# An adaLN block on one core: two row sums a head with six carried tiles, division inside the attention, a shorter preparation and a projection without GpSimd

## The reference, cut to what matters

```python
mod = (silu(c) @ wmod).reshape(B, 6, 1, -1)          # sa, ca, ga, sb, cb, gb; ga and gb kept away from 0
h = layernorm(x) * (1 + ca) + sa                     # x: 2 x 2048 x 512
mixed = h @ Wqkv.T                                   # q, k, v of 16 heads of 32, per batch: 32 heads
attn = softmax(q @ k.T * 32 ** -0.5)                 # 2048 x 2048 for each of the 32 heads
x = x + ga * ((attn @ v) @ Wproj.T + bproj)
h = layernorm(x) * (1 + cb) + sb
hidden = fwht(silu(h @ W1.T) * (h @ W3.T))           # 2048 wide
x = x + gb * (hidden @ W2.T)
```

## Time and profile before

| | us |
|---|---|
| median of three runs | 3419.07 (3417.18 to 3424.57) |
| the profiled execution, its own time | 3422.99 |
| its span, first to last instruction | 3421.2 |
| busy: PE, DVE, ACT, POOL | 3173.1, 1892.1, 1534.8, 1588.4 |
| prepare and entry of project_qkv, up to its first matmul | 109.5 |
| project_qkv, matmuls | 283.5 |
| attend, from the last projection to its first score | 67 |
| attend, 31 heads | 1607 |
| attend, last head, which sums by PE | 65 |
| gap to the first matmul of project_out | 25 |
| project_out | 186 |
| feed_forward | 1078 |

### The profile page before, as it was taken

How to read it: one execution, slowest core, us unless ns; L and a number is a source line. 1 busy time by engine, 2 the same in 40 slices (tenths; PEclk the granted TensorE clock), 3 DMA queues, 4 the chain that set the end, 5 groups by cost and what they waited for, 6 DMA issues and landing times. The chain is left out here.

```text
span 3421.2 us, 48695 instructions
## 1 busy us (share of the span) xinstructions
PE 3173.1 (93%) x15340; PEld 2114.3 (62%) x15340; DVE 1892.1 (55%) x3144; ACT 1534.8 (45%) x2869; POOL 1588.4 (46%) x566
## 2 busy tenths in 40 slices
PE   5899799999999999999999998667999999999998
PEld 3688555545555555545555552456888888888887
DVE  5443398778777777777777780653333233223232
ACT  3333146666666666656666665233322222222221
POOL 5000059999888998989989992540000000000000
PEclk7999879999999999999999999878999999999999
DMA  5556537877777777777777763854221121121111
GB/s 213 163 164 183 157 67 166 173 161 163 167 156 168 160 162 157 158 165 162 160 159 163 166 135 76 245 189 164 84 83 47 56 71 44 57 70 44 59 56 34
DMA packets 150990, 446.92 MB, mean 131 GB/s; under 512 B 27398, under 2 KB 45062, under 8 KB 116044
## 3 DMA queue, kind: packets, MB, share of 16 engines
q0 software_dynamic: 28064, 199.24, 28.9%
q1 hardware_dynamic: 122668, 244.39, 24.6%
HBM read 167.78 MB, written 80.23 MB: 72 GB/s over the span
## 5 line engine op out<-in xcount | busy, mean ns | idle before, releaser
L1009 DVE TENSOR_REDUCE mxp<-pmax 128x1 f32<-128x512 f32 x2048 | 1258.9, 681 | 373.3 <-PE pmax L830 372.8
L966 ACT ACTIVATE prob<-pexp 128x512 f32<-128x512 f32 x2048 | 1037.9, 623 | 576.5 <-PE pexp L875 491.0
L830 PE MATMUL pmax<-kst,qst 96*128 96x512 f32 x2048 | 870.7, 433 | 41.4 <-issue 21.0
L1066 POOL TENSOR_TENSOR gsum<-gsum,prob 128x2048 f32<-128x2048 f32 x186 | 877.6, 4718 | 17.9
L875 PE MATMUL pexp<-qst,kst 98*128 98x512 f32 x2048 | 827.9, 424 | 45.2 <-ACT prob L966 45.2
L830 PEld LDWEIGHTS pmax<-kst,qst 96*128 96x128 f32 x2048 | 407.7, 199 | 327.1 <-DVE mxp L1009 184.1
L875 PEld LDWEIGHTS pexp<-qst,kst 98*128 98x128 f32 x2048 | 399.8, 196 | 246.5 <-ACT prob L966 174.3
L1066 POOL TENSOR_TENSOR gsum<-prob 128x2048 f32<-128x2048 f32 x93 | 472.0, 5076 | 76.9 <-ACT prob L966 76.9
L884 PE MATMUL pctx<-prob,v 128*32 128x512 f32 x4096 | 498.2, 603 | 0.0
L1642 DVE TENSOR_TENSOR hid<-sil,pl 128x512 f32<-128x512 f32 x128 | 88.0, 688 | 638.6 <-PE pl L51 631.6
L51 PE MATMUL pg<-h2f,w 128*128 128x512 f32 x1536 | 371.1, 391 | 1.1 <-issue 1.1
(11 more groups left out here) (109 smaller groups left out, 1757.6 us busy)
## 6 DMA issues: line engine op xcount, KB each, us to landing
gsum<-prob POOLq DMA_DIRECT2D x124, 1024.0 KB, 9.7
gsum<-gsum POOLq DMA_DIRECT2D x62, 1024.0 KB, 8.5
w<-w_scratch SPq DMA_DIRECT2D x128, 256.0 KB, 2.6
qst<-q_scratch SPq DMA_DIRECT2D x96, 256.0 KB, 6.4
kst<-k_scratch SPq DMA_DIRECT2D x96, 256.0 KB, 7.2
xin<-in_L_attn_query_dram SPq DMA_DIRECT2D x16, 1024.0 KB, 8.5
q_scratch<-obq SPq DMA_DIRECT2D x32, 512.0 KB, 5.0
k_scratch<-obq SPq DMA_DIRECT2D x32, 512.0 KB, 3.6
```

The lines of the kernel that those rows point to most:

```text
L830: pe.matmul(pmax[:, bank, :], qst[0:KR, slot, qt * P:(qt + 1) * P], kst[0:KR, slot, kc * TOK:(kc + 1) * TOK], start=True, stop=True).then_ ...
L966: act.activation(prob[:, kt % RING, j * TOK:(j + 1) * TOK], pexp[:, score_bank(r, n), :], ACT.Exp, scale=SCALE).then_inc(exp_done, 1)
L1009: dve.tensor_reduce(mxp[:, par, u // QJ, u % QJ:u % QJ + 1], pmax[:, bank, :], X, ALU.max).then_inc(mx_done, 1)
L1066: pool.tensor_tensor(dst, a, prob[:, kt % RING, :], ALU.add).then_inc(add_done, 1)
```

## The change: what it does

- **Row sums.** Two buffers for a head instead of three, each kept for two heads. POOL does eight adds (tiles 0 to 4, and 5, 6, 8, 9, 11), six tiles (7, 10, 12, 13, 14, 15) are carried by DMA, to the buffers 0, 0, 1, 0, 1, 0, and nothing is merged: PE runs `unit` on both buffers, after the fifth burst.
- **Order.** `M` and `q` alternate strictly. `INVERT_AT` goes from 44 to 20. The loop over heads is written out on all engines.
- **Division.** SP broadcasts the reciprocals to `recb` and POOL multiplies the contexts of head g-2 in `divide`; SP stores them after that. The last head is divided by DVE, from PSUM. `project_out` loads no reciprocals any more.
- **Preparation.** The whole rows of Wqkv come in four transfers, nothing of W2 is done, low parts are made by DVE from PSUM, tokens of tile 0 are turned there. The transform of W2 goes into `project_qkv`: POOL loads a quarter and does 8 butterflies of 128x1024, PE turns 16 blocks and does 4 Hadamard matmuls, in tiles 0, 2, 4 and 6 (`fold_turn` after result 9, `fold_mult` after result 11).
- **project_out** has no POOL work: the bias is a two-row matmul at the end of each result.

```diff
+                load_rows(0)
+                load_rows(1)
+                load_tokens(sp, ins, keep["xin"], 0, 0).then_inc(keep["x_in"][0], 16)
+                load_rows(2)
+                load_rows(3)
+                load_mod(0)
+                load_mod(1)
+                sp.dma_start(natp[:, :, :], ins["wproj"].rearrange("(j p) n -> p j n", p=P)).then_inc(natp_in, 16)
+                load_mod(2)
+                load_mod(3)
+                sp.dma_start(had[:, :], ins["hadamard"]).then_inc(keep["had_in"], 16)
+                load_tokens(sp, ins, keep["xin"], 0, 1).then_inc(keep["x_in"][1], 16)
...
+                def fold_mult(s, b):
+
+                    n = FOLD_AT.index(2 * s + b)
+                    pe.wait_ge(keep["had_in"], 16)
+                    for i in range(DC):
+                        pe.wait_ge(w2_taken, DC * n + i + 1)
+                        pe.matmul(pt[:, i, :], had[:, :], wt[:, i * D:(i + 1) * D], start=True, stop=True).then_inc(w2_mm, 1)
...
+                for n in range(DC):
+                    if n:
+                        pool.wait_ge(w2_turned, DC * n)
+                    pool.dma_start(wn[:, :], ins["w2"][n * P:(n + 1) * P, :]).then_inc(w2_in, 16)
+                    if n:
+                        pool.wait_ge(w2_scaled, DC * n)
+                        pool.dma_start(scratch["w2"][:, :, (n - 1) * P:n * P].rearrange("c p n -> p c n"),
+                                       wt[:, :].rearrange("p (c n) -> p c n", c=HC)).then_inc(w2_out, 16)
+                        pool.wait_ge(w2_out, 16 * n)
+                    pool.wait_ge(w2_in, 16 * (n + 1))
+                    for m in range(2 * STAGES):
...
-ORDER = "MqMqMqMqMqMqqMqM"
-POOLED = ((0, 1, 2, 3), (5, 6, 7, 8), (11, 12, 13, 15))
-CARRIED = (4, 9, 10, 14)
-MERGES = 6
+ORDER = "Mq" * 8
+POOLED = ((0, 1, 2, 3, 4), (5, 6, 8, 9, 11))
+CARRIED = (7, 10, 12, 13, 14, 15)
+UNITS = len(POOLED)
 ADDS = sum(len(g) - 1 for g in POOLED)
-TURN_AFTER, UNIT_AFTER = 48, 55
-INVERT_AT = 44
+TURN_AFTER, UNIT_AFTER = 48, 39
+INVERT_AT = 20
...
-        late[UNIT_AFTER // 8].append(("unit", 0))
+        late[UNIT_AFTER // 8] += [("unit", k) for k in range(UNITS)]
...
+    CARRY_TO = (0, 0, 1, 0, 1, 0)
...
+                def spread_rec(g):
 
                     sp.wait_ge(inverted, g + 1)
-                    sp.dma_start(scratch["rec"][bass.ds(g, 1), :].rearrange("o (p n) -> (o p) n", p=P),
-                                 recc[:, par, :]).then_inc(rec_out[par], 16)
+                    sp.dma_start(scratch["rec"].rearrange("(p n) -> p n", p=P), recc[:, :]).then_inc(rec_out, 16)
+                    sp.wait_ge(rec_out, 16 * (g + 1))
+                    if g:
+                        sp.wait_ge(divided, g)
+                    for j in range(QJ):
+                        sp.dma_start(recb[j * HD:(j + 1) * HD, :], scratch["rec"][j * TOK:(j + 1) * TOK]
+                                     .partition_broadcast(HD)).then_inc(rec_in, 16)
 
...
-                    par = (r - 1) % 2
-                    if exists(g - 1):
-                        if exists(g + 3):
+                    if exists(g + 3):
+                        if exists(g - 1):
                             sp.wait_ge(pv_done, KT * g)
-                            load(g + 3, (r + 3) % SLOTS)
-                        store_ctx(g - 1, par, i * 2 + (r - 1) // 2)
-                    else:
                         load(g + 3, (r + 3) % SLOTS)
                     if exists(g - 2):
-                        fetch_sum(g - 2, r % 2, i * 2 + (r - 2) // 2 + 1)
+                        fetch_sum(g - 2)
+                        spread_rec(g - 2)
+                    if exists(g - 1):
+                        store_sum(g - 1)
                     if exists(g + 1):
                         max_row(g + 1, (r + 1) % SLOTS)
                     if exists(g - 2):
-                        store_rec(g - 2, r % 2)
-                    if exists(g - 1):
-                        store_sum(g - 1, par)
+                        store_ctx(g - 2)
+                    if g == 1:
...
+                    k, kt = CARRY_TO[i], CARRIED[i]
                     exp_ready(g, kt)
+                    before = [n for n in range(i) if CARRY_TO[n] == k]
+                    if before:
+                        pool.wait_ge(merged[before[-1]], 16 * (g + 1))
+                    else:
+                        pool.wait_ge(add_done, ADDS * g + adds_until(POOLED[k][-1]))
+                    pool.dma_start(group_sum(k, g), prob[:, kt % RING, :], accum_op=ALU.add).then_inc(merged[i], 16)
+
+                def divide(g):
+
+                    pool.wait_ge(ctx_read, g + 1)
+                    pool.wait_ge(rec_in, 16 * QJ * (g + 1))
+                    pool.tensor_tensor(ctxo[:, g % OUT, :], ctxo[:, g % OUT, :], recb[:, :], ALU.mult).then_inc(divided, 1)
                 def head(g):
 
+                    for m in (1, 2, 3, 4):
+                        add(g, 0, m)
+                    carry(g, 0)
+                    add(g, 1, 1)
+                    add(g, 1, 2)
+                    carry(g, 1)
+                    add(g, 1, 3)
+                    add(g, 1, 4)
+                    carry(g, 2)
+                    carry(g, 3)
                     if g >= 2:
-                        pool.wait_ge(unit_done, g - 1)
-                    add(g, first_sum(g), 0, 1)
-                    if g:
-                        join_second(g - 1)
-                    add(g, first_sum(g), 0, 2)
-                    add(g, first_sum(g), 0, 3)
-                    if g:
-                        join_third(g - 1)
-                    pool.wait_ge(add_done, ADDS * g + adds_until(POOLED[0][-1]))
-                    carry(g, first_sum(g), 4)
-                    if g >= 2:
-                        pool.wait_ge(merged[4], 16 * (g - 1))
-                    for m in (1, 2, 3):
-                        add(g, second_sum(g), 1, m)
-                    pool.wait_ge(add_done, ADDS * g + adds_until(POOLED[1][-1]))
-                    carry(g, second_sum(g), 9)
-                    pool.wait_ge(merged[0], 16 * (g + 1))
-                    carry(g, first_sum(g), 10)
-                    if g:
-                        pool.wait_ge(merged[5], 16 * g)
-                    add(g, third_sum(), 2, 1)
-                    add(g, third_sum(), 2, 2)
-                    pool.wait_ge(merged[2], 16 * (g + 1))
-                    carry(g, first_sum(g), 14)
-                    add(g, third_sum(), 2, 3)
-
+                        divide(g - 2)
+                    carry(g, 4)
+                    carry(g, 5)
...
-                    pe.wait_ge(c_hi, DC * (t + 1))
-                    pe.wait_ge(c_lo, DC * (t + 1))
                     for k in range(TK):
                         if t:
                             pe.wait_ge(scaled, TK * t + k + 1 - TK)
-                        split_product(pe, po[:, k, :], lambda a, c: cs[:, t % 2, a, c, k * P:(k + 1) * P],
-                                      lambda a, c: wp[:, a, c, :], range(DC)).then_inc(mm, 1)
+                        for c in range(DC):
+                            if k == 0:
+                                pe.wait_ge(c_hi, DC * t + c + 1)
+                                pe.wait_ge(c_lo, DC * t + c + 1)
+                            split_product(pe, po[:, k, :], lambda a, c: cs[:, t % 2, a, c, k * P:(k + 1) * P],
+                                          lambda a, c: wp[:, a, c, :], (c,), start=(c == 0), stop=False)
+                        pe.matmul(po[:, k, :], ones[:, :], bias[:, :], start=False, stop=True).then_inc(mm, 1)
 
                 def turn(t):
...
-                def scale_ctx(t):
-                    pool.wait_ge(ctx_in[t % 2], 16 * (t // 2 + 1))
-                    pool.wait_ge(rec_in[t % 2], 4 * RECS * (t // 2 + 1))
-                    for c in range(DC):
-                        pool.tensor_tensor(cin[:, t % 2, c, :], cin[:, t % 2, c, :], rb[:, t % 2, c, :],
-                                           ALU.mult).then_inc(c_scaled, 1)
-
-                def bias(t):
-                    pool.wait_ge(x_in[t % 2], 16 * (t // 2 + 1))
-                    for k in range(TK):
-                        pool.tensor_tensor(xin[:, t % 2, k, :], xin[:, t % 2, k, :], gains[:, 1, t // ST, :],
-                                           ALU.add).then_inc(x_bias, 1)
-
```

More of the change, by code:

```diff
@@ new lines, in _, with high, out_high @@
+            @block.scalar
+            def _(act):
+                def high(j):
+                    act.wait_ge(row_pe, j + 1)
+                    for t in range(QKV):
+                        src, (hi, _) = part(j, t)
+                        act.activation(hi, src, ACT.Copy).then_inc(row_hi, 1)
+                def out_high(j):
+                    act.wait_ge(out_pe, j + 1)
+                    src, (hi, _) = out_part(j)
+                    act.activation(hi, src, ACT.Copy).then_inc(out_hi, 1)
@@ new lines, in turn_tokens, with normal_tokens @@
```

(46 more changed lines are left out.)

698 lines of the change are left out of this document (317 added, 381 removed).

## The result

The changed kernel takes 3615.91 us (median of four executions, 3608.84 to 3619.74) beside 3420.63 of before: a ratio of 1.0568, 95% interval 1.0547 to 1.0589, slower by 5.7%. The forecast was 3463 with a range to 3545, so the direction is right and the time 71 us above the range.

What follows compares the result with a forecast made beforehand. POOL's round of adds and carry landings was taken to bound the heads. Preparation -61, project_qkv +21, heads +142, project_out -50 and gap -7.5 gave +44.5 us: 3463 on the median of 3419.07, range 3350 to 3545.

Steps and rivals of the forecast that it cites:

- The other stages: Outside the heads: preparation -61 us, project_qkv +21, project_out -50, gap ahead of it -7.5.
- POOL's round: Heads: POOL's adds, carries and waits for landings set the head, 54.6 us, or 57.1 with the loads.
- the collision: Heads: the next head's loads in flight delay carry 13's landing, 2.5 us a head, bounds 0 and 4.5.
- a rival: Heads: the loads miss carry 13, 54.6 us a head, 3393 in all; chance 0.20.
- DVE takes the wait: Heads: DVE waits 10 us for `sumc` before maximum 20, PE stands 7; 56.4 a head, 3443; chance 0.11.
- the ring: Heads: `prob` has eight tiles, so the next head's exponential tile 7 waits for carry 15; 57.1 us a head.
- the backlog: Heads, DVE's wait rival: 1 us a head added to PE's 48.3 and its 7 us stand.
- the chain: Heads: POOL's carry 14 waits for 12's landing, 15 for 13's; 10 of 12.2 us behind no work.
- what would show it: Heads: POOL idle about 10 us before the fourth carry, second carries landing after 12 to 15, ACT waiting at tiles 4 to 7.
- The fast rival: Heads: carry 13 lands 7 us after issue, POOL does not fall behind, PE bounds; 3233 in all; chance 0.20.

Runs made afterwards that it cites:

- the kernel with late loads: Changed kernel, with SP fetching sums and spreading reciprocals first and issuing the next head's seven loads after them: 3430.4 us (1.0025).
- the best: The kernel with late loads, plus tile 14 carried, tile 15 summed by PE ahead of the buffers, reciprocal before maximum 32: 3259.2 us (0.9532).
- Without the tail: Changed kernel with sums asked for ahead of the loads, without the carries of tiles 14 and 15 (row sums incomplete): 3216.7 us (0.9407).
- 3278 and 3280: The kernel with late loads, plus tiles 14 and 15 summed by PE: reciprocal before maximum 20, 3278.1 us; before maximum 32, 3280.4 us.

## Why the prediction was right or wrong

**The other stages** came within 5 us in sum (-92.9 for -97.5). First projection matmul at 49.4 (forecast 48), project_qkv 304.0 (304), gap 14.3 (17.5; DVE's reciprocal 3.36, and the load 5 instead of 7). Only the tiles were mis-sized: 117.7 for 110. Their bound is PE, as forecast, but a bias matmul of two rows takes 0.43 us between its neighbours' starts, twice the 0.22 that I took, and 12 matmuls 2.94, so a tile with its turn is 4 x 3.37 + 1.72 = 15.2 us where it was put at 13.9 (and eight times 13.9 is 111, not the 108 of the prediction; in the 117.7 us stand eight tiles and five of the eight turns):

```profile
2455.51 1.97 PE L1281 MATMUL pt<-ident,xn 128*128 128x128 f32 x16
2457.23 2.99 PE L51 MATMUL po<-wp,cs 128*128 128x512 f32 x12
2460.16 0.50 PE L1273 MATMUL po<-bias,bias_ones 2*128 2x512 f32 x1
2460.58 3.02 PE L51 MATMUL po<-wp,cs 128*128 128x512 f32 x12
```

**POOL's round** was right as a mechanism, and as a size where it could be seen: 54.6 forecast, 55.3 measured with DVE's wait and the collision both away; 57.1 forecast with the loads, 57.1 measured with DVE's wait away. The second agreement is partly luck. The second carry of a pair landed after 13.0 to 14.2 us in these kernels, where 12.2 was taken. The loads were to fall on carry 13; they fell on 14 and 15, which the forecast had only as an argument against a rival, and the cycle then ran through ACT's tile 7. The collision was 1.9 us a head, 2.5 in the forecast.

**DVE's wait** is where it failed. The step is the price of the rival "DVE takes the wait": 56.4 us a head, under the ring's 57.1 and so with a chance of 0.11. The runs show 61.2. Its terms were short: SP's loads issued in 6 us, as in the kernel before (measured 10.1; 5.7 without carries 14 and 15), so that `sumc` came later and DVE's wait was 13.7 instead of 10; PE's stall 10.7 instead of 7; and 1 us for the backlog where the lower clock took some 2. The landing of 12.2 was right (12.5). With these numbers the rival's own sum, 48.3 + 10.7 + 2, is 61.0.

The sentence "It falls at the same tiles as the ring's wait, so the two do not add" held: in the changed kernel only DVE's wait is left (371.7 us against 2.5 of ACT for carries), and in the kernel with late loads DVE's 5.8 us cost nothing beside the chain. What it left out is that one wait lengthens the other: the forecast took SP's issues from the kernel before, and in the changed kernel carries 14 and 15 are in flight beside them. So the head's 12.9 us over the floor of 48.3 has no division into two shares that stand by themselves: a later reciprocal takes 4.1 off it, leaving out the two last carries 8.1, and leaving them out with the sums asked for ahead of the loads all 12.9. The range failed with it: it left out what lies a little above 60 us a head, and 61.2 lies there.

**Of what would show it**: POOL did not stand 10 us for a DMA by the page, which named ACT; ACT waited for carries only once DVE's wait was gone, at tiles 6 and 7 with the loads beside them and, with late loads and the reciprocal at 32, at 5 and 7 in the head shown; second carries landed after 13.0 to 14.2 us, within the 12 to 15 given. The profile after thus spoke against the mechanism though it was there, and only the experiment brought it out.

**The fast rival** (3233) had the right floor, 48.4, and needed what the change lacked: no chain behind the last tiles. Without the tail, and with the sums ahead of the loads, the kernel takes 3216.7; with the row sums in full, the best took 3259.2.

## What to carry to other kernels

Two waits that end at the same place do not add, but when both depend on DMAs each has to be priced with the other's transfers in flight, and only then is the longer one taken. A round trip through DRAM should be waited for late in an in-order queue: waiting late cost nothing (3278 and 3280), and waiting early cost 59 to 127 us wherever DVE's wait was the longer one; and the last links of a chain of accumulating DMAs belong on an engine that works in order anyway, here 0.95 us of PE for a tile against a landing of 9 to 17. After taking one wait away, profile again: what the first profile names is the wait that ends last, not the only one.

## What the runs showed of the hardware that I had not expected

- An 8 KB transfer of SP's lands in 1.7 us alone, in 6.5 beside the end of two carries, in 7.8 right behind the loads with the carries landed, and in 12 to 13 while carries of 1 MB issued by POOL are in flight, even ahead of the loads, or with the loads cut to 2 KB (11.8). Four stores of contexts (64 KB each) stand right ahead of it in SP's queue in these last kernels, but they do so too where it landed in 6.5.
- SP's issue of a load takes 0.42 to 0.45 us once the carries have landed. While carries are in flight it takes mostly 1.2 to 1.9 us in the changed kernel and its variants (the first of a series can take 0.3), also for transfers of 2 KB; in the kernel before it took 1.0 (2.88/3) beside one carry:

```profile
1027.97 5.07 SPq L797 DMA_DIRECT2D qst<-q_scratch  x3
```

(with the loads cut to 16 columns), against, with the loads moved behind the landing of carry 15 (issued at 1035.28, landed 9.1 us later):

```profile
1046.36 1.35 SPq L796 DMA_DIRECT2D qst<-q_scratch  x3
```

What holds SP there, its own queue or something shared with POOL's, no run tells apart.
- Carries of 1 MB (14 and 15), issued 6.6 us apart beside 1.8 MB of loads, land 15.7 and 17.1 us after their issue; with the loads cut to 2 KB, issued 7.3 us apart, 12.4 and 10.0.
- A two-row matmul of 512 columns costs 0.43 us among its neighbours, where a 128-row one of the same width costs 2.94/12 = 0.25.
